# Linear-attention blocks on one Trainium2 core: seven float32 products of a step written as sums of three products of rounded parts, with a new order on every engine

## What is computed

```python
for i in range(NUM_BLOCKS):                      # 8
    residual = x
    Q = fmap(x @ Wq[i] + bq[i])                  # fmap(t) = elu(t) + 1
    K = fmap(x @ Wk[i] + bk[i])
    value = x @ Wv[i] + bv[i]
    KV = jnp.einsum('nsh,nsh->nh', K, value)
    Ksum = jnp.sum(K, axis=1)
    Z = 1.0 / (Q * Ksum[:, None, :] + EPS_ATTN)
    V = Q * KV[:, None, :] * Z
    attn_out = gelu(V @ Wo[i] + bo[i])
    x = _ln(attn_out + residual, ln1_s[i], ln1_b[i])
    residual = x
    h = gelu(x @ W1[i] + b1[i])                  # 128 -> 512
    ff_out = gelu(h @ W2[i] + b2[i])             # 512 -> 128
    x = _ln(ff_out + residual, ln2_s[i], ln2_b[i])
```

## Time and profile before

| | us |
|---|---|
| median of three runs | 3519.7 |
| lowest and highest run | 3518.75 and 3526.47 |
| span of the profiled execution | 3506.0 |
| in it, by the timeline and roughly: both attentions, with their routing | 0 to 1180 |
| experts and collecting of their rows | 1180 to 1751 |
| linear blocks | 1751 to 3345 |
| ternary layer | 3345 to 3506 |

### The profile page before, as it was taken

How to read it: one execution, slowest core, us unless ns; L and a number is a source line. 1 busy time by engine, 2 the same in 40 slices (tenths; PEclk the granted TensorE clock), 3 DMA queues, 4 the chain that set the end, 5 groups by cost and what they waited for, 6 DMA issues and landing times. The chain is left out here.

```text
span 3506.0 us, 72683 instructions
## 1 busy us (share of the span) xinstructions
PE 3144.6 (90%) x22614; PEld 1680.9 (48%) x22614; DVE 2452.0 (70%) x6945; ACT 2276.8 (65%) x3088; POOL 1534.6 (44%) x1807
## 2 busy tenths in 40 slices
PE   6999995898988884987299999999999999999978
PEld 2555552454544452554144444444444444444456
DVE  4666655888777752332678888888888888888754
ACT  4777771555555562222678888888888888888723
POOL 3444442345455523565634333444333444433443
PEclk9999995899999996999599999999999999999989
DMA  4444443222222212443300000000000000000001
GB/s 100 119 118 103 108 100 84 55 61 64 66 53 54 64 40 66 126 142 101 106 7 0 9 0 9 0 9 0 3 6 2 7 0 9 0 9 0 0 16 34
DMA packets 173142, 162.16 MB, mean 46 GB/s; under 512 B 18276, under 2 KB 156735, under 8 KB 172830
## 3 DMA queue, kind: packets, MB, share of 16 engines
q1 hardware_dynamic: 163838, 142.35, 16.7%
q0 software_dynamic: 9088, 16.88, 1.4%
HBM read 92.40 MB, written 68.52 MB: 46 GB/s over the span
## 5 line engine op out<-in xcount | busy, mean ns | idle before, releaser
L546 ACT ACTIVATE ga_PT<-ga_S 128x1024 f32<-128x1024 f32 (+1 forms) x384 | 336.3, 880 | 286.2 <-PE ga_S L373 283.0
L2717 POOL TENSOR_TENSOR lb_y<-lb_ao,XC 128x512 f32<-128x512 f32 x128 | 163.2, 1275 | 807.3 <-ACT lb_ao L2664 807.3
L2556 PE MATMUL lb_H<-lb_x,lb_w 128*128 (+1 forms) x1024 | 513.8, 604 | 0.5 <-issue 0.5
L2565 PE MATMUL lb_FF<-lb_h,lb_w 128*128 128x512 f32 x1024 | 460.3, 592 | 0.0
L2671 ACT ACTIVATE lb_h<-lb_H,lb_prm 128x512 f32<-128x512 f32 x512 | 351.7, 687 | 99.8 <-PE lb_H L2556 84.7
L2763 DVE TENSOR_SCALAR lb_z<-lb_M,lb_mv,lb_rstd 128x128 f32<-128x128 f32 x1024 | 349.9, 404 | 32.8 <-POOL lb_rstd L2708 9.4
L2565 PEld LDWEIGHTS lb_FF<-lb_h,lb_w 128*128 128x128 f32 x1024 | 194.6, 190 | 244.9 <-issue 215.4
L2708 POOL TENSOR_TENSOR lb_rstd<-lb_rstd,half 128x4 f32<-128x4 f32 x256 | 259.5, 1014 | 37.0 <-issue 0.2
L2755 DVE BATCH_NORM_STATS2 lb_stats<-lb_M 128x6 f32<-128x128 f32 x1024 | 228.3, 285 | 30.9 <-PE lb_M L2538 23.0
L2556 PEld LDWEIGHTS lb_H<-lb_x,lb_w 128*128 128x128 f32 x1024 | 174.0, 190 | 132.3 <-issue 122.8
L1521 POOL TENSOR_SCALAR_AFFINE_SELECT da_PT<-da_PT 128x1024 f32<-128x1024 f32 x128 | 146.1, 1146 | 196.3 <-ACT da_PT L1451 196.3
(11 more groups left out here) (330 smaller groups left out, 7087.7 us busy)
## 6 DMA issues: line engine op xcount, KB each, us to landing
moe_w<-experts_dram SPq DMA_DIRECT2D x39, 384.0 KB
da_qT<-da_stq SPq DMA_DIRECT2D x64, 192.0 KB, 4.3
da_kT<-da_stk SPq DMA_DIRECT2D x64, 192.0 KB, 5.2
ga_qT<-ga_stq SPq DMA_DIRECT2D x32, 384.0 KB, 6.0
moe_x<-moe_xs SPq DMA_DIRECT2D x39, 258.0 KB
tc_g<-moe_ys SPq DMA_DIRECT2D x32, 256.0 KB, 3.2
da_stq<-da_parts SPq DMA_DIRECT2D x16, 384.0 KB, 2.4
da_stk<-da_parts SPq DMA_DIRECT2D x16, 384.0 KB, 3.1
```

Of the source, the lines that this page charges most:

```text
L546: act.activation(PT[:, n % RING, :, lo:hi], score_banks(u)[:, :, 0:hi - lo], ACT.Exp, scale=SCALE).then_inc(probs, 1)
L2556: pe.matmul(H[:, k % 2, :], w1[:, k, :], x1_of(i), start=True, stop=True).then_inc(h_filled, 1)
L2565: pe.matmul(FF[:, :], w2[:, k, :], h[:, k, :], start=(k == 0), stop=(k == KC - 1)).then_inc(ff_filled, 1)
L2717: pool.tensor_tensor(y1[:, :], ao[:, :], state(i), ALU.add).then_inc(y1_ready, 1)
```

## The change

In the linear blocks the seven products Q, K, V and up (four times) of a step are no longer float32 products. Each operand is split in a high part, its copy in the type float32r, and a remainder, the operand less its high part, in float32r too. A product becomes high x high + high x low + low x high, three float32r products of 512 columns summed in PSUM. The product with Wo and the four down products stay float32.

The weights are split once, in the expert stage: after each odd tile from 3 on, one block's `bqkv` and `bw1` (128x896) get a copy on ScalarE and a subtraction on VectorE, and both parts go to a DRAM tensor `split`, from which `linear_blocks` loads tiles twice as large. The operands that move are split on GpSimd in the linear blocks: `high_of_state` and `low_of_state` make `xs` of the state, one step ahead, and `split_x1` makes `x1s` of `x1`; that is two copies and two subtractions of 128x512 in a step. V's semaphore and H's now say when `xs` and `x1s` may be written again. The steps g = 15 and g = 127 are written out.

The order of a step is new on four engines. ScalarE takes K's exponential ahead of Q's, and `ao` ahead of the write-back. TensorE takes K, Q, the transposes of z1, V, the last down product of the sequence before, Wo, then the up products in their parts, with the transposes of z2, y2 and y1 among them, and three down products at the end. What VectorE and GpSimd do is in the excerpts of the order behind the diff.

```diff
+            def high_part(k):
+                act.wait_ge(raw_loaded[k % 2], 32 * (k // 2 + 1))
+                if k >= 2:
+                    act.wait_ge(parts_stored[k % 2], 16 * (k // 2))
+                act.activation(parts[:, k % 2, 0, :, :], raw[:, k % 2, :, :], ACT.Copy
+                               ).then_inc(high_ready, 1)
...
+            def low_part(k):
+                v.wait_ge(high_ready, k + 1)
+                v.tensor_tensor(parts[:, k % 2, 1, :, :], raw[:, k % 2, :, :],
+                                parts[:, k % 2, 0, :, :].bitcast(F32), ALU.subtract
+                                ).then_inc(low_ready, 1)
...
+                if block_at(j) is not None:
+                    store_parts(block_at(j))
+                    if block_at(j) + 2 < NBLK:
+                        load_raw(block_at(j) + 2)
...
-        wqkv = sb("wqkv", [P, 3, P])
+        wqkv = sb("wqkv", [P, 2, 3, P], F32R)
...
+        xs = sb("xs", [P, 2, 2, SEQ], F32R)
+        x1s = sb("x1s", [P, 2, SEQ], F32R)
...
-                part(g, g >= NB, lambda k: 0 <= g - k < NG)
+                part(g, g + 1 >= NB, lambda k: 0 <= g - k < NG)
             for g in range(5):
                 fixed(g)
-            with eng.Fori(5, NB) as g:
+            with eng.Fori(5, NB - 1) as g:
                 part(g, False, lambda k: True)
-            with eng.Fori(NB, NG) as g:
+            fixed(NB - 1)
+            with eng.Fori(NB, NG - 1) as g:
                 part(g, True, lambda k: True)
+            fixed(NG - 1)
...
+            def project(W, i, out, signal):
+
+
+                pe.matmul(out, wqkv[:, 0, W, :], part_of_x(i, 0), start=True, stop=False)
+                pe.matmul(out, wqkv[:, 0, W, :], part_of_x(i, 1), start=False, stop=False)
+                pe.matmul(out, wqkv[:, 1, W, :], part_of_x(i, 0), start=False, stop=True
+                          ).then_inc(signal, 1)
...
+            def project_k(g):
                 pe.wait_ge(wqkv_loaded, 16 * block_of(g) + 16)
-                if old:
-                    pe.wait_ge(x_ready, g - NB + 1)
+                pe.wait_ge(xs_ready, g + 1)
+                if reused(g):
+                    pe.wait_ge(fk_ready, g)
+                project(1, g, K[:, :], k_filled)
...
-            def up(i, k):
+            def up_high(i, k):
                 if k == 0:
                     pe.wait_ge(w1_loaded, 16 * block_of(i) + 16)
-                    pe.wait_ge(x1_ready, i + 1)
+                    pe.wait_ge(x1_high_ready, i + 1)
                     if reused(i):
-                        pe.wait_ge(h_ready, KC * i)
+                        pe.wait_ge(h_ready, KC * i - 1)
+                if k == 1 and reused(i):
+                    pe.wait_ge(h_ready, KC * i)
                 if k >= 2:
                     pe.wait_ge(h_ready, KC * i + k - 1)
-                pe.matmul(H[:, k % 2, :], w1[:, k, :], x1_of(i), start=True, stop=True
+                pe.matmul(H[:, k % 2, :], w1[:, 0, k, :], x1s[:, 0, :], start=True, stop=False)
+                pe.matmul(H[:, k % 2, :], w1[:, 1, k, :], x1s[:, 0, :], start=False, stop=False)
+
+            def up_low(i, k):
+                if k == 0:
+                    pe.wait_ge(x1_low_ready, i + 1)
+                pe.matmul(H[:, k % 2, :], w1[:, 0, k, :], x1s[:, 1, :], start=False, stop=True
                           ).then_inc(h_filled, 1)
...
             def part(g, old, on):
                 if on(0):
-                    project_q(g, old)
+                    project_k(g)
+                    project_q(g)
                 if on(2):
                     turn_z1(g - 2)
                 if on(0):
-                    project_k(g)
                     project_v(g)
-                if on(5):
-                    turn_z2(g - 5)
+                if on(3):
+                    down(g - 3, KC - 1)
                 if on(1):
                     attention_out(g - 1)
                 if on(2):
-                    up(g - 2, 0)
-                    up(g - 2, 1)
+                    up_high(g - 2, 0)
+                if on(5):
+                    turn_z2(g - 5)
+                if on(2):
+                    up_low(g - 2, 0)
+                    up_high(g - 2, 1)
+                    up_low(g - 2, 1)
                 if on(4):
                     turn_y2(g - 4)
-                if on(2):
-                    up(g - 2, 2)
                 if on(1):
                     turn_y1(g - 1)
                 if on(2):
-                    up(g - 2, 3)
-                    for k in range(KC):
+                    for k in range(2, KC):
+                        up_high(g - 2, k)
+                        up_low(g - 2, k)
+                    for k in range(KC - 1):
                         down(g - 2, k)
...
+            def high_of_state(i, old):
+                if reused(i):
+                    if old:
+                        pool.wait_ge(x_ready, i - NB + 1)
+                    pool.wait_ge(v_filled, i - 1)
+                pool.tensor_copy(part_of_x(i, 0), state(i))
+
+            def low_of_state(i):
+                pool.tensor_tensor(part_of_x(i, 1), state(i), part_of_x(i, 0).bitcast(F32),
+                                   ALU.subtract).then_inc(xs_ready, 1)
+
+            def split_x1(i):
+                pool.wait_ge(x1_ready, i + 1)
+                if reused(i):
+                    pool.wait_ge(h_filled, KC * i)
+                pool.tensor_copy(x1s[:, 0, :], x1_of(i)
+                                   ).then_inc(x1_high_ready, 1)
+                pool.drain()
+                pool.tensor_tensor(x1s[:, 1, :], x1_of(i), x1s[:, 0, :].bitcast(F32), ALU.subtract
+                                   ).then_inc(x1_low_ready, 1)
+
             def part(g, old, on):
+                if on(-1):
+                    high_of_state(g + 1, old)
+                if on(2):
+                    split_x1(g - 2)
                 if on(1):
                     i = g - 1
                     pool.wait_ge(ao_ready, i + 1)
                     if reused(i):
                         pool.wait_ge(y1_turned, i)
                     pool.tensor_tensor(y1[:, :], ao[:, :], state(i), ALU.add).then_inc(y1_ready, 1)
-                if on(4):
-                    rsqrt_stats(g - 4, stats2_ready, mv2, rstd2, rstd2_ready)
+                if on(-1):
+                    pool.drain()
+                    low_of_state(g + 1)
...
+                if on(4):
+                    rsqrt_stats(g - 4, stats2_ready, mv2, rstd2, rstd2_ready)
...
-                        v.wait_ge(h_filled, KC * i - KC)
...
-                    sp.dma_start(wqkv[:, :, :], C["bqkv_dram"][k].rearrange(
-                        "p (c n) -> p c n", c=3)).then_inc(wqkv_loaded, 16)
+                    sp.dma_start(wqkv[:, :, :, :].bitcast(F32), R["split"][k][:, :, 0:3, :]
+                                 ).then_inc(wqkv_loaded, 16)
```

119 lines of the change are left out of this document (74 added, 45 removed).

## The result

The changed kernel takes **3543.6 us** (3540.0 to 3545.5 in four runs) beside 3522.2 for the kernel before (3518.8 to 3526.5): a ratio of **1.0058, 95% interval 1.0044 to 1.0073**. It is slower, by 21 us, where 149 was forecast. Its profiled execution has a span of 3540.1, 34 more than that of before, and some of this is in stages whose code is the same: the expert stage begins 10.1 later (first transposes of a tile at 1406.4 instead of 1396.3).

A forecast was written before the change was run, and what follows sets the result against it. TensorE bounds the linear blocks at 12.26 us a step; afterwards VectorE's 11.3 plus 2.1 of stalls gives 13.4. 123 x 1.15 = 141, plus 8, on 3506.0 gives 3655, plus 13.7 gives 3669 us; range 3450 to 3690.

The forecast's parts named there:

- The exclusion: Linear blocks: GpSimd and VectorE's clips or `att` exclude each other for a whole streamed instruction; `fk` and `kv` pass.
- Who is first: After `x1`: GpSimd's subtraction starts at 1.06, `ek` at 1.32 inside it, so `ek` ends +0.88 later.
- the 11.3 without a hindrance: VectorE's linear step without any new hindrance: 11.3 us, making VectorE the bound, with at most 0.96 us a step to win.
- my 13.4: Linear step in us with clips blocked: 11.3 plus stalls of 0.88, 1.10 and 0.15; 1.15 more than now.
- the second rival: Linear step: only one clip blocked, one stall of 1.1; 12.4 us a step, 3545 us (3520 to 3565); chance 0.22.
- the third rival: Linear step: both clips pass before `y1` or escape the exclusion; 11.7 us a step, 3459 us (3430 to 3500); chance 0.32.
- the signs named ahead: Linear stage: right if clips exceed 1 us, TensorE is about 80% busy, step 13.4; wrong if clips 0.42, step under 12.
- TensorE's step: Linear blocks: seven products as three rounded ones at 0.65, five float32 at 0.86, four transposes at 0.44: 10.6 us, 1.5 less.
- the ring: Study's linear-step cycle: `x1`, its copy and remainder, `y1`, transposes, statistics, `z1`, transposes, next `x1`; 6.06 plus 6.34 us measured.
- The rest: Outside the 123 full steps: expert-stage loads 3, first linear weights 1, ten edge steps 4; together +8 us.
- The range: Whole kernel: 3450 to 3690 us, with chances of faster 0.33, within measurement precision 0.05, slower 0.62.
- the fourth rival: Linear step, costlier arithmetic: GpSimd copies at 1.50 (3595 us) or two-pass rounded products, 15.1 a step (3870); chance 0.11.

The follow-up runs named there:

- With GpSimd winning by 0.02 more: The changed kernel with a tiny VectorE memset (128x8) between the centring of z2 and the clip of `ek`: 3647.9 us, ratio 1.0391 to before.
- the TensorE-bound kernel (11.15): The changed kernel with all 128 linear steps written out on every engine and the clip of `ek` ahead of z2's centring: 3338.8 us, ratio 0.9667 to before.
- the kernel nearest to it: The changed kernel with all 128 linear steps written out on every engine instead of two loops: 3398.0 us, ratio 0.9686 to before.

## Why the prediction was wrong, step by step

**The exclusion: right.** A streamed GpSimd instruction and a fast SBUF-to-SBUF clip (or `att`, with two SBUF inputs, beside which the copy of the state took 1.04 and not 0.61) exclude each other for whole instructions; `fk` and `kv` pass. The 8-column clip of 1.26 us shows it best. The forecast's row for `fk` did not show this: `fk` ended at 2607.36, before `y1` started at 2607.81. The changed kernel does: `fk` runs from 2602.87, inside the long subtraction, and keeps its 0.75.
The Trainium skill (SBUF — State Buffer, SBUF: two separate sides) says that whichever starts first gets the pair for the whole instruction. The trace agrees with the whole instruction, but not quite with the first start: by the profile's records GpSimd's was 0.07 to 0.08 ahead, and VectorE had the access in nearly all steps.

**Who is first: the step that failed.** The forecast had, from `x1`'s end, the subtraction at 1.06 and `ek` at 1.32, a margin of 0.26 for GpSimd. Measured by the same mark (0.73 after `x1`'s start): 1.19 and 1.27. On GpSimd's side 0.13 went: the copy starts 0.40 after `x1`'s end, where the forecast had 0.3, and 0.14 in steps written out, so the addresses computed in the loop cost it. On VectorE's side it was 0.05: `ek` starts at 1.27 and not 1.32 (the forecast's sum for the step has 1.40 for the same four centrings). What is left of the margin, 0.08, is where it tips: GpSimd wins every step only from 0.087 on. I had named the risk ("the margins are 0.2 to 0.3 us") and gave it to rivals whose conditions (a copy of 0.9 or more, `y1` 0.3 later) were not the ones that happened.

**What a loss costs GpSimd: not considered.** I counted only stalls of VectorE. When VectorE wins, GpSimd waits: 0.68 in the subtraction (for `ek` and `eq` back to back, VectorE keeping the access between them) and 0.20 in `y1`. That goes through `y1`'s transposes to VectorE's statistics, a wait of 1.23. So the step is 12.40, between the 11.3 without a hindrance and my 13.4. The number is that of the second rival (12.4 and 3545), but by luck, since the mechanism is not: that one had a clip stalled by 1.1, and here, but for two steps, no clip stalls by more than 0.1. It is not the third rival's either, though the clips pass there: it has the exclusion cost nothing, and here it costs GpSimd. So the signs named ahead met neither side: clips at 0.42, as in "wrong", and a step above 12.

**The size.** 1.0 us in nearly every one of 123 steps is 123 us, and the forecast lies 125 above the result. With GpSimd winning by 0.02 more, the kernel took 1.0391 of before; the forecast's 3669 on 3519.7 is 1.0424. There the clips stall by 1.04 and 1.09, where the forecast had 0.88 and 1.10. TensorE's busy share at that step is 90% (358.49 of 400), and not about 80%.

**TensorE's step.** Forecast 10.6, by three rounded products at 0.65. They are 0.235 apart, so 0.70 for three:

```profile
2609.97 0.39 PE L2554 MATMUL lb_K<-lb_xs,lb_wqkv 128*128 x1
...
2610.20 0.40 PE L2555 MATMUL lb_K<-lb_xs,lb_wqkv 128*128 x1
...
2610.44 0.39 PE L2553 MATMUL lb_Q<-lb_xs,lb_wqkv 128*128 x1
```

Seven times 0.05 is 0.35 of the 0.55 by which the TensorE-bound kernel (11.15) lies above 10.6. The copy of `x1` at 0.61 was right to the hundredth, and so was `x1`, 0.52 after the end of z1's transposes (2611.78 to 2612.30). For the copy of the state 0.61 was too little (1.04), but it is not on the ring. The 11.3 for VectorE without hindrance can't be held against a row of its own; the kernel nearest to it has 11.27, with addresses gone.

**The rest.** +8 forecast. The expert stage cost 3.9 (3 forecast), and elsewhere 8.7, where TensorE had no idle time without the split. From the last `x1` to the last write-back it is 34.5 instead of 25.9: 8.5 for the steps that let the pipeline run empty, where 4 was forecast for all ten edge steps. The ternary layer behind it was 3.0 shorter with unchanged code (154.2 and 151.2; another trace of before has 151.6), so to the end it is 5.6. The granted clock was 1.00 in the window shown, as assumed. Of the 34 us between the two spans, 14.5 are the linear steps, 5.6 what follows the last `x1`, 3.9 the expert stage and 10.1 stages with unchanged code.

**The range.** 3450 to 3690 holds 3543.6, and slower was right; what was wrong is the likeliest case and with it the size, 21 where 149 was forecast. Two slips of arithmetic changed nothing in it: half of 2.86 is 1.43 and not 1.46, and the fourth rival's 15.1 a step makes 3877 and not 3870.

## What to carry to other kernels

Where two engines exclude each other for whole instructions, a forecast must give both outcomes of each meeting and their margins in hundredths of a microsecond; a margin under 0.1 says nothing about who wins, and the loser's delay counts even when the loser is the idle engine. Before an order is judged, move the short instruction out of the meeting (one clip a few lines up was worth 1.5%), and look at loops whose addresses are computed in registers: they shift every start; written out, they gave 0.8% on the kernel before and 2.5% on the one with `ek` moved. Less work on one engine can cost time, if it lets that engine reach the shared access first.

## What the runs showed of the hardware

- An access shared by VectorE and GpSimd is granted for a whole instruction: a clip of 8 columns behind a GpSimd subtraction took 1.26 us. A full clip that starts 0.063 to 0.078 us after GpSimd's instruction, by the profile, still has it; from 0.087 us on GpSimd has it; between them it goes either way. Two clips back to back keep it between them (0.68 us of delay).
- A float32r product of 512 columns takes 0.235 us of TensorE's queue at full clock, three of them 0.70, against 0.86 for one float32 product.
- The kernel before took 3452 on one chip and 3522 on another. In two of its traces, 52.8 us apart, 49.6 of these stand ahead of the linear blocks, 26.6 in the expert stage (243.7 and 217.1).
- With its steps in a loop, its addresses in registers, GpSimd started its copy 0.26 us later after `x1` than with them written out (1.13 and 0.87). With the loops of the other engines the part of the ring behind the statistics was 0.64 longer.
- In the changed kernel a VectorE instruction that reads PSUM and one SBUF tensor kept its 0.75 us beside a GpSimd subtraction.
